# A top-4 router beside attention: logits from rows not yet normed, and the last but one tile routed within the closing steps

## The reference, cut to what matters

```python
h = _rms(x, ln_w)                      # x * rsqrt(mean(x*x) + 1e-5) * ln_w
q, k, v = h @ wq, h @ wk, h @ wv       # 32 heads of 64, 8 key heads
q, k = _rope(q, k)
attn = softmax(causal(q k^T / 8), -1)
x = x + (attn v) @ wo
h = _rms(x, ff_ln_w)
logits = h @ wg                        # 16 experts
topv, topi = top_k(logits, 4)
gate = softmax(topv, -1)
a = silu(h @ w1[e]) * (h @ w3[e])      # for each chosen expert e
moe = sum over e of gate[e] * (a @ w2[e])
return x + moe
```

## Time and profile before

| | before |
|---|---|
| median of 3 runs | 3807.46 us (3806.72 to 3809.56) |
| the profiled execution's own time | 3817.35 us |
| its span in the profile | 3815.6 us |
| busy, PE / PEld / DVE / ACT / POOL | 3340.4 / 2195.9 / 2627.6 / 1932.8 / 993.4 us |
| mean granted clock of PE | 0.918 of full speed |
| stretch of the first attention's last column group, and the tail behind it | about 640 to 936 us |
| the same of the second attention | about 2440 to 2732 us |

### The profile page before, as it was taken

One profiled execution on the slowest core, in us unless ns is written; L12 is line 12 of the kernel. 1 busy time (PEld: TensorE's weight loads), 2 busy tenths in 40 slices (PEclk: granted clock), 3 DMA queues, 4 the chain that ended last, 5 costly groups with the idle time before them and its releaser, 6 DMA issues. The chain is left out here.

```text
span 3815.6 us, 62869 instructions
## 1 busy us (share of the span) xinstructions
PE 3340.4 (88%) x21000; PEld 2195.9 (58%) x21002; DVE 2627.6 (69%) x8701; ACT 1932.8 (51%) x5261; POOL 993.4 (26%) x960
## 2 busy tenths in 40 slices
PE   6999999986995898998799999988699558999975
PEld 4666666653553433343567666765355347878864
DVE  6888888874443766774788888877344467777766
ACT  4667676653221355666466767665222115555531
POOL 3212121333443000011221212134344333222213
PEclk9999999997997678999899999998799769999986
DMA  4231300013654222110242310001565500000010
GB/s 125 78 136 55 112 1 1 33 48 122 150 90 100 65 47 56 43 29 17 74 132 82 110 58 1 1 34 59 158 121 88 127 14 15 1 15 4 1 33 23
DMA packets 201926, 234.63 MB, mean 61 GB/s; under 512 B 20358, under 2 KB 188232, under 8 KB 200776
## 3 DMA queue, kind: packets, MB, share of 16 engines
q1 hardware_dynamic: 170664, 190.48, 16.4%
q0 software_dynamic: 30944, 40.14, 6.2%
HBM read 98.13 MB, written 133.73 MB: 61 GB/s over the span
## 5 line engine op out<-in xcount | busy, mean ns | idle before, releaser
L1732 ACT ACTIVATE p_prob<-bank,p_small 128x256 f32<-128x256 f32 (+3 forms) x1280 | 647.4, 516 | 170.7 <-DVE p_small L1903 166.1
L1903 DVE CUSTOM_DVE_ANT_0 bank<-bank,p_mask 128x256 f32<-128x256 f32 (+3 forms) x1280 | 578.5, 489 | 93.5 <-PE bank L1475 82.6
L2248 POOL TENSOR_TENSOR p_tm<-p_rope_a,p_rope_b 128x512 f32<-128x512 f32 x192 | 246.5, 1284 | 1324.2 <-DVE p_rope_b L1883 1319.8
L1475 PE MATMUL bank<-p_k,p_q 64*128 64x256 f32 (+3 forms) x3840 | 528.0, 347 | 18.5 <-ACT p_prob L1732 17.3
L1737 ACT ACTIVATE p_prT<-bank 128x512 f32<-128x512 f32 x752 | 425.1, 601 | 197.7 <-PE bank L1484 196.3
L1484 PE MATMUL bank<-g_ident,p_prob 128*128 128x128 f32 x3008 | 440.2, 286 | 43.7 <-DVE p_prob L1912 18.8
L1912 DVE TENSOR_SCALAR p_prob<-p_prob,p_small 128x256 f32<-128x256 f32 (+3 forms) x1280 | 414.2, 387 | 11.3
L1493 PE MATMUL bank<-p_prT,p_v 128*64 128x512 f32 (+1 forms) x1504 | 420.4, 606 | 0.3 <-ACT p_prT L1737 0.3
L1484 PEld LDWEIGHTS bank<-g_ident,p_prob 128*128 128x128 f32 x3008 | 333.2, 143 | 138.6 <-issue 56.2
L1475 PEld LDWEIGHTS bank<-p_k,p_q 64*128 64x128 f32 (+1 forms) x3840 | 338.3, 188 | 119.8 <-issue 63.0
L1949 DVE TENSOR_REDUCE p_nmax<-bank 128x1 f32<-128x512 f32 x512 | 325.0, 684 | 108.7 <-PE bank L1534 103.4
(11 more groups left out here) (289 smaller groups left out, 6253.6 us busy)
## 6 DMA issues: line engine op xcount, KB each, us to landing
sorted<-p_blank SPq DMA_DIRECT2D x32, 2304.0 KB, 19.2
p_w<-in_L_ffn_w SPq DMA_DIRECT2D x96, 256.0 KB, 4.4
p_h_in<-sorted SPq DMA_DIRECT2D x158, 144.0 KB, 2.7
p_k_st<-k_saved SPq DMA_DIRECT2D x16, 288.0 KB
p_q_st<-q_saved SPq DMA_DIRECT2D x16, 288.0 KB
g_stage<-in_L_ffn_wq SPq DMA_DIRECT2D x8, 512.0 KB, 4.4
g_stage<-in_L_ffn_wo SPq DMA_DIRECT2D x16, 256.0 KB, 5.1
g_res<-first_sum SPq DMA_DIRECT2D x8, 512.0 KB, 7.2
```

What stands on the lines that cost most here:

```text
L1475: ins = pe.matmul(h.use.ap[:, 0:n], q[rows, at, :], k[rows, kp, o.g, keys], start=i == 0, stop=i == 2)
L1732: act.activation(s.prob.ap[:, 0:s.o.w], s.use.ap[:, 0:s.o.w], ACT.Exp, bias=sm[:, 0, j:j + 1], scale=-1.0, accum_out=sm[:, 1, j:j + 1]).th ...
L1903: dve.tensor_tensor_reduce(x, x, A.mask[:, A.mask.shape[1] - o.w:], -1.0, FAR, ALU.add, ALU.min, o.sm.ap[:, 0, h.j:h.j + 1]).then_inc(made)
```

## The change: what it does

1. The routing's transposes read the residual itself (`route_square`, PE); `route_mean`, `route_root`, `route_scale` and `route_turn` are gone as steps. Mean and root (POOL) are made beside the logits.
2. The norm's weight is multiplied into the router's matrix once (`router_weights`, DVE); for that it is loaded as a column, by a second DMA at the very start.
3. The root goes into the exponential as its scale, one instruction for each tile, and the exponentials (ACT) and the scaling of the rows (DVE) move into `route_place`.
4. In the last batch, tiles 12 and 13 wait for one call where they waited for three, and tile 14 for none where it waited for three (pairs of earlier batches keep three); behind the last unit `route_on` is called between the closing steps, so that tile 14 is routed there.
5. The tables of the experts are emitted behind the last tiles' routing.

```diff
         self.step("router", R)   # in router(), ahead of it:
+        if not self.wg_scaled:
+            self.step("router_weights")
+            self.wg_scaled = [self.vector_made.up() for _ in range(KC)]
...
-                    routing.append(self.route(self.routed, list(done), wring, 0 if (o.b, o.t) == (B - 1, T - 1) else 3))
+                    routing.append(self.route(self.routed, list(done), wring, 3 if o.b < B - 1 else 1 if o.t < 2 else 0))
...
+        while len(routing) > 1:
+            route_on()
+        route_on()
         normalise(prev)
+        route_on()
         for kt in range(prev.nkt):
             turn(prev, kt)
-        project_out(low_parts(weigh(pend + [prev])))
+            if kt < 3:
+                route_on()
+        weighed = low_parts(weigh(pend + [prev]))
+        route_on()
+        project_out(weighed)
+        route_on()
...
+        for e in range(4):
+            weights(e)
+        pieces = self.routing
+        for _ in pieces:
+            pass
         s = self.step("expert_tables", A)
...
-        elif s.kind == "route_turn":
-            w.wait_ge(s.use.before, s.ready)
-            for t, x in enumerate(s.slots):
+        elif s.kind == "route_square":
+            w.wait_ge(s.use.before, *s.ready)
+            for t, i in enumerate(s.tiles):
                 for k in range(KC):
-                    ins = pe.transpose(s.use.ap[:, (t * KC + k) * P:(t * KC + k + 1) * P], x.ap[:, k * P:(k + 1) * P], ident[:, :])
+                    ins = pe.transpose(s.use.ap[:, (t * KC + k) * P:(t * KC + k + 1) * P], plan.res[:, i, k * P:(k + 1) * P], ident[:, :])
...
-        elif s.kind == "route_pick":
-            w.wait_ge(s.less)
-            act.activation(A.ex[:, 0:s.n, :], A.ex[:, 0:s.n, :], ACT.Exp).then_inc(made)
+        elif s.kind == "route_place":
+            for t in range(s.n):
+                w.wait_ge(s.less, s.rooted)
+                act.activation(A.ex[:, t, :], A.ex[:, t, :], ACT.Exp, scale=A.rs[:, t:t + 1]).then_inc(made)
...
+        elif s.kind == "router_weights":
+            w.wait_ge(plan.wg_loaded)
+            for k in range(KC):
+                dve.tensor_scalar(plan.wg[:, k, :], plan.wg[:, k, :], plan.wg_norm[:, k:k + 1], None, ALU.mult).then_inc(made)
...
         elif s.kind == "route_place":
             n = s.n
+            for t, i in enumerate(s.tiles):
+                w.wait_ge(s.rooted, A.lnw_loaded)
+                dve.scalar_tensor_tensor(s.slots[t].ap[:, 0:D], plan.res[:, i, :], A.rs[:, t:t + 1], A.lnw,
+                                         ALU.mult, ALU.mult).then_inc(made)
             w.wait_ge(s.use.full, s.counted, s.place.after)
...
-        elif s.kind == "route_root":
+        elif s.kind == "route_logits":
             n = s.n
             w.wait_ge(s.padded, s.after, own.turn())
             pool.tensor_tensor(A.rs[:, 0:n], A.ms[:, 0:n], plan.half[:, 0:n], ALU.pow).then_inc(made)
...
             sp.dma_start(plan.wg[:, :, :], chunks(io["L0_ffn_wg"])).then_inc(s.wg_count.sem, 16)
+            sp.dma_start(plan.wg_norm[:, :], io["L0_ffn_ff_ln_w"].rearrange("(c p) -> p c", p=P),
+                         allow_slow_non_contiguous=True).then_inc(s.wg_count.sem, 16)
```

66 lines of the change are left out of this document (27 added, 39 removed).

## The result

| | before | after |
|---|---|---|
| median | 3807.09 us (3806.52 to 3809.56, 4 runs) | 3771.85 us (3755.09 to 3772.66, 4 runs) |
| ratio to before | 1 | 0.9893, 95% interval 0.9868 to 0.9918 |
| the profiled execution's own time, its span | 3817.35, 3815.6 us | 3755.09, 3753.3 us |

The account below looks back on a forecast made before the run. PE was taken as the bound, losing time only in waits and slow clock. An attention: 15 + 12 - 1 + 13 = 39 us; two, less 1.1, give 77: 3807.46 becomes 3730 us, 8-in-10 range 3708 to 3760.

Parts of the forecast that it names:

- Units A to D: Two last-column-group units routing tile pairs (0,1) to (6,7): 7.5 us gained each as PE's waits and slow clock go.
- Rival 1: PE's waits are handed on to rank, turns and scores behind DVE's placing burst; gain only 47 us, 3760; chance 0.20.
- The last unit, 12 - 1 = 11: Unit routing the last three pairs: 7.5 us of waits plus 4.5 of clock gained, less 1 for routing tile 14.
- G's wait of 1.8 us: In the last unit, transposes of pair (12,13) directly behind tile 13's projection wait some 1.8 us for DVE's sum.
- The tail, 13: Last residual sum to first expert transpose, only tile 15 left to route: 13 us gained (10 to 14).
- part 2: Tile 14 routed within the closing steps behind the last unit; cost 1 us (0 to 2.5).
- part 1: Routing transposes read the residual, square, mean, root and scale off PE's path; 7.5 us a unit, 12 in the last.
- The start, 1.1: Loading the norm's weight as a column by a second small DMA costs 1.1 us once (0.5 to 3).
- Rival 4: Slower: DVE's scaling and ACT's exponentials wait for POOL's root behind scatters, up to 122 us; 3853; chance 0.04.

Follow-up runs that it names:

- f4: Changed kernel, its waits of 3 calls kept, but ACT scales the rows, not DVE, norm's weight left out of them; median 3748.41 us.
- e1: Changed kernel, but pairs of the first three batches wait for 7 calls in place of 3, putting the placing back; median 3758.94 us.
- e6: Changed kernel with waits of 7 calls and rows scaled by ACT, not DVE, norm's weight left out of them; median 3758.43 us.
- e3: Changed kernel, but ACT copies the transposed rows ahead of its squares of the residual; median 3774.05 us.
- e4: Changed kernel, but with the old closing steps: the rest of the routing of tiles 12 to 14 is emitted in the experts; median 3779.97 us.
- e7: Changed kernel, but the weights of experts 1 to 3 are loaded behind the first four block loads; median 3764.76 us.
- e8: Changed kernel with waits of 7, 7, 3 calls, ACT's copy ahead of its squares, the norm weight's column loaded later; median 3763.21 us.
- f1: Changed kernel, ACT scaling rows, norm's weight in experts' copy, its column and experts 1 to 3 weights later, waits 7, 7, 2 and 5, 7, 3; median 3754.31 us.
- f3: Changed kernel, DVE still scaling, with the norm weight's column and weights of experts 1 to 3 loaded later, waits of 5, 7, 2; median 3760.38 us.
- g2: Changed kernel, ACT scaling rows, norm's weight in experts' copy, column and experts 1 to 3 weights later, pair waits 7, 5, 7, 5, 2, 2; median 3740.57 us.
- g3: As g2, but for tiles 8 to 15 ACT copies the transposes ahead of its squares; median 3734.99 us.
- e2: Changed kernel, but the placing frees the ranks' bank directly behind the positions and scales the rows last, same DVE work; median 3763.90 us.

## Why the prediction was wrong, by its steps

- **Units A to D, 15 us an attention: the step that failed.** The 4.63 us waits went, as did the clock behind them (priced at about 1 us, 1.4 in fact). Wrong was to take 7.5 of a unit's 10.3 us of waits and slow clock as gone and to add nothing in their place. Cut on PE, unit 1 gained 0.0 and unit 2 0.9 and 1.1 us; the lead took 1.1 more. In the first attention three waits for the rows, 10.3 us together, went from the two units, and PE stands still only 3.4 us less: it waits 8.0 us for the placing instead of 2.3, and 1.7 for the choice instead of none. The low clock cost 1.1 and 1.6 us more there, not less. I had asked how full DVE is, and taken that only as an upper bound; the question was what its burst, moved four calls ahead and longer by the scaling, would stand beside. Cut on PE, the scaling out of DVE gives 2.1 to 3.8 us a unit (f4), the placing put back 0.7 to 3.6 (e1), both together 2.5 to 5.9 (e6).
- **Rival 1 named this mechanism** (waits handed on to what stands behind the burst) and priced a unit at 3.5 us of gain, so even it was too kind there (its 5 us for the last unit were near). Its whole, 47 us, is nearer to the measured 35 than the forecast's 77. It took the burst as 2.7 us, as its parts add up alone; beside a rope sum the two scalings alone cost 1.0 us more.
- **The last unit, 12 - 1 = 11: the clock about right, the waits wrong.** Cut on PE it gained 6.8 and 5.7 us. The slow clock gave 5.4 and 4.6 back where 4.5 were taken. Of the 7.5 us of waits (net) only 1.4 and 1.2 us showed: by so much less PE stands still. The rows took 6.3 us there, not 7.3: E's 1.0 lies in unit 2. And 4.2 us were kept, where the trace has 4.5 for the choice, 2.4 for ACT's copy, 2.2 for residual sums and 1.2 for placings. G's wait of 1.8 us is 1.69, as said. Missed: F waits 2.44 us for ACT's copy, which stands behind two squares, and 2.54 for the choice, where I had kept 0.7 and 0.3; G waits 1.34 and tile 14 0.62 for theirs. The copy put ahead of the squares gives 1.7 and 1.1 us of it back (e3).
- **The tail, 13: right in size (11.9 and 12.4), wrong in its reason.** From the last sum to the first scatter it is 6.84 us (907.04 against 900.20), near the forecast's 7.2 (913.3 against 906.06), and the weights cost 2.6 us behind it, where I took 1. But 9 of the 12 us would have come without part 2 (e4): my sum never asked how the tail looks with part 1 alone.
- **The start, 1.1: 0.6, and not told apart from nothing.** The second DMA took 0.45 us to issue, and 1.6 of the first 2.1 us of delay were made up before the fifth tile's sum. But the last sum of the third column group starts at 670.1 to 671.3 us in the changed kernel, e1 to e7 and f4, which load the column at the start, and at 669.8 to 671.8 in e8, f1 to f3, g2 and g3, which load it later.
- **Rival 4 (slower)** did not happen: no scaling in the units waited for a root; the one that did is tile 15's, behind four scatters, as forecast:

```profile
904.81 0.58 POOL L2326 TENSOR_TENSOR p_n_tiles<-p_n_tiles,g_minus_half 128x1 f32<-128x1 f32 x1
905.42 0.48 DVE L2088 SCALAR_TENSOR_TENSOR p_row<-g_res,p_n_tiles 128x256 f32<-128x256 f32 x1 [1.55 <-POOL p_n_tiles L2326]
```

- **The Trainium skill, "TensorE: Matmul & The Clock Gate"**, in "What's actually happening", would have left 13 us of clock gain out of my sum, which gives a gain of 64. The trace stands between the two: in the last unit 5.4 and 4.6 us came back, in the units 1.1 and 1.6 were lost, so an attention gave 4.3 and 3.0 us back where 6.5 were forecast and none by that rule. What failed more was that waits, and spells with them, came back elsewhere.

## What to carry to other kernels

- A step that is shortened moves all behind it. Before pricing the wait that goes, ask of each burst that moves what it will stand beside: who is queued behind it on its engine, and what POOL does meanwhile.
- A wait that is met at a bank or a buffer is not priced there: freeing the bank (e2) moved most of its 8 us to later turns (5.0 of them to the rope products), taking the work away (f4) gained.
- A stretch that is cut at an instruction of one engine also measures how late that engine is: cut where the engine that is priced ends the same work.
- Before a gain is given to one part of a change, work the place out with each part alone.
